# Image stores of the weight stage: twelve pieces, one in each of steps 6 to 17, in place of six in a row

## The chip, the core and the metric

The kernel runs on one core of one Trainium2 chip. The metric is the device time of one execution in microseconds (us), from the first to the last instruction of the program. Three timed executions of the kernel before gave 1593.47, 1605.23 and 1599.48 us, a median of 1599.48 us.

## What is computed

A tower of three layers on 16 images of 3 x 112 x 112. Only the first layer, the patch tokenizer, touches the change. Cut to what matters here:

```python
# x: 16 x 3 x 112 x 112 -> 784 patches of 3 x 16 x 16
x = (x - mean) / (1e-06 + std)           # per patch and colour, ddof=1
x = x / sqrt(16)
x = conv2d(x, conv1_w, conv1_b)          # 3 -> 64 channels, 3x3
residual = x
x = gelu(group_norm(x, gn1_g, gn1_b))
x = conv2d(x, rconv1_w, rconv1_b)        # 64 -> 64
x = gelu(group_norm(x, gn2_g, gn2_b))
x = conv2d(x, rconv2_w, rconv2_b)        # 64 -> 64
x = residual + x
x = conv2d(x, proj_w, proj_b, stride=16) # 64 x 16 x 16 -> 192: one token per patch
tokens = x + row_emb[...] + col_emb[...]
# then an attention layer and a two-branch transformer layer on the tokens
```

The last 3x3 convolution is linear and is followed by a linear projection, so the kernel folds rconv2_w into proj_w once, before it touches a patch. It also folds the projection with conv1_w, for the residual path.

## The kernel before

The program has three stages: the **weight stage** (the first 246 us), the **patch stage** (conv1, norm, gelu, conv, norm, gelu and projection over 784 patches, two in flight, in seven groups), and the tail with the attention and transformer layers. Each engine runs its own stream of instructions, and the streams meet at semaphores.

**The weight stage** folds 192 output channels in 24 steps (FU = 24) of 8 channels (U = 8). Step n works in one of two halves of everything, p = n % 2. In the order in which the data go through it:

- SyncE (SP), `fold_io` (L227): waits until VectorE has split step n's weights (`s_psp`, L230), loads the projection weights of step n + 2 into the stage that this frees (`load_proj`, L215 and L216: `sb_f32q` for even steps, a part of `sb_arena` for odd ones), waits until ScalarE has evacuated step n's second product (`s_tev`, L232), and stores it to DRAM (`scratch_fold`) with two DMAs (L234).
- VectorE (DVE), `proj_split` (L675): waits for the load, and for TensorE to be through with step n - 2 (`s_tps`, L679); writes the weights as an fp16 high part (L682) and an fp16 rest (L684) into `sb_acts`.
- TensorE (PE), `fold_step` (L504): waits for the split of step n (L506), does 36 matmuls of 512 columns (L476) and 18 of 192 columns (L517).
- ScalarE (ACT), `fold_step` (L389): moves the results out of PSUM (L393, L400).
- VectorE, `w_lo` (L686, L691): the low part of the folded weights. On VectorE the order is w_lo of step n - 2, split of step n, w_lo of step n - 1, split of step n + 1 (`fold_pair`, L709). Its first splits and its work on the image (L700 to L735) stand among them.

Two buffers hold the weights on their way in, two the split weights, two each result.

**The image** is loaded once as `xt` (112 partitions, 3 colours, 7 patches of 256 numbers, fp32), normalised by VectorE in place (`s_xch` counts to 42), and split into 12 padded fp16 planes `xhl`, 6 of high parts and 6 of rests (`s_xhl` counts to 13). SyncE writes both back to DRAM. `xt` goes to `scratch_x` with three DMAs (L244), one for each colour. `xhl` goes to `x_planes` with three DMAs (L247) of six planes each: high parts, rests, high parts again. Eight small DMAs (L252) then store zeros from `sb_arena` behind the last patch of the 18 planes. All fourteen count up `s_scr`. When it has its full 14 x 16 (L263), SyncE reads the first patches back with `load_im` (L254, L256), for units 0 and 1, two DMAs each, into `sb_im`. VectorE waits for the same count at L757 before it lets the patch stage reuse the image's buffers.

**Order on SyncE before.** The queue is one stream, written out by hand: `fold_io` of steps 0 to 5 as a hardware loop (`Fori(0, 3)`), then the six image stores and the eight zero stores in a row, then `fold_io` of steps 6 to 21 as a second hardware loop, then the wait on `s_scr` and the four loads of `sb_im`, then `fold_io` of steps 22 and 23 without a load, then the store of the low weights (L269), and then the patch stage.

TensorE starts the patch stage with `conv1` (L535, L536) after waits on `s_im`, on VectorE's memsets of first rows (`s_rowz`, L763), and on the last evacuations of the weight stage (L629 to L634). It needs unit 1 in `sb_im` at the third conv1 (L638).

Of the kernel before, what the change touches and what calls it, by code (L numbers as in the profile page):

```python
# [22 lines left out]
B, C, P, CH, E = 16, 3, 16, 64, 192  # L23
HP = 7
ROWS = B * HP
NPAT = ROWS * HP
SL, WD = 9, 18
PAD = SL * WD
# [7 lines left out]
FU = E // U  # L36
RUN = (U - 1) * PAD + 8 * WD + P
PLANE = (NPAT + 3 * U + 1) * PAD
# [11 lines left out]
W_READY = 10  # L50
HB = U * PAD + WD
MID = 48
MEANS_AT, CONV1_AT = 10, 13


# [14 lines left out]
def build_front(nc, a, emb, xs, ts, wrd):  # L70
# [7 lines left out]
    scr = nc.dram_tensor("x_planes", (18, PLANE), F16)  # L78
    wlod = nc.dram_tensor("w_lo", (128, HALF * E), F16)
    with ExitStack() as ctx:  # L80
# [3 lines left out]
        def sem(name):  # L84
            return ctx.enter_context(nc.semaphore(name))
# [46 lines left out]
        n = 2 * C * 7 * 256  # L132
        xt = b0[0:ROWS, 0:n].bitcast(F32).rearrange("p (c w n) -> p c w n", c=C, w=7)
        xhl = b0[0:ROWS, n:n + 12 * 7 * PAD].rearrange("p (q n) -> p q n", q=12)
# [26 lines left out]
        s_cst, s_xvar, s_xstd, s_xz, s_xhl, s_xch = (sem("constants"), sem("x_var"), sem("x_std"), sem("x_zeroed"),  # L161
                                               sem("x_split"), sem("x_chain"))
        s_scr, s_zero, s_padz = sem("x_stored"), sem("zero_tile"), sem("pads_zeroed")
# [42 lines left out]
        def _(sp):  # L206
# [8 lines left out]
            def load_proj(n, p):  # L215
                sp.dma_start(stage[p], a["proj"][:, bass.ds(n * (U * DENSE), U * DENSE)]).then_inc(s_pld[p], 16)  # L216
# [10 lines left out]
            def fold_io(i, p, last):  # L227
                n = 2 * i + p
                if not last:
                    sp.wait_ge(s_psp, 2 * n + 2)  # L230
                    load_proj(n + 2, p)
                sp.wait_ge(s_tev, 3 * n + 3)  # L232
                for h in range(2):
                    sp.dma_start(bass.AP(tensor=ts.tensor, offset=n * (U * TR * DENSE) + h * (Q * TR * DENSE),  # L234
                                         ap=[[DENSE, TR], [TR * DENSE, Q], [1, DENSE]]),
                                 tev[p][TP * h:TP * h + TR, :, :]).then_inc(s_ts[p], 16)

            with sp.Fori(0, 3) as i:
                for p in range(2):
                    fold_io(i, p, False)  # L240

            sp.wait_ge(s_xch, 42)
            for c in range(C):
                sp.dma_start(xs.rearrange("(r w) (c n) -> r c w n", w=7, c=C)[:, c], xt[:, c]).then_inc(s_scr, 16)  # L244
            sp.wait_ge(s_xhl, 13)
            for k, h in enumerate((0, 1, 0)):
                sp.dma_start(bass.AP(tensor=scr, offset=k * 6 * PLANE, ap=[[7 * PAD, ROWS], [PLANE, 6], [1, 7 * PAD]]),  # L247
                             xhl[:, 6 * h:6 * h + 6, :]).then_inc(s_scr, 16)
            sp.wait_ge(s_zero, 1)
            for n, k in ((NPAT, U), (NPAT + U, U), (NPAT + 2 * U, U), (NPAT + 3 * U, 1)):  # L250
                for at, planes in ((0, 12), (12, 6)):
# [2 lines left out]
            def load_im(u, p):  # L254
                for up in range(2):
                    sp.dma_start(im[p][54 * up:54 * up + 54, 0:RUN],  # L256
                                 bass.AP(tensor=scr, offset=u * (U * PAD) + up * WD,
                                         ap=[[1, 3], [PLANE, 18], [1, RUN]])).then_inc(s_im[p], 16)

            with sp.Fori(3, FU // 2 - 1) as i:  # L260
                for p in range(2):
                    fold_io(i, p, False)
            sp.wait_ge(s_scr, 16 * 14)  # L263
            load_im(0, 0)
            load_im(1, 1)
            for p in range(2):
# [201 lines left out]
        def _(pe):  # L468
# [79 lines left out]
            def project(b, n0, n1):  # L548

                for n in range(n0, n1):  # L550
                    c = max(k for k in range(NCH) if CHS[k] <= n)
                    to_low = (HALF + (c % 2) * WCH + n - CHS[c] - n) * E
                    both = bass.AP(tensor=wall, offset=n * E, ap=[[WALL, 128], [to_low, 2], [1, E]])
                    tiles = ((0, 0), (64, MID))
                    for at, k in tiles:
# [96 lines left out]
        def _(dve):  # L652
# [13 lines left out]
            n = 4  # L666
# [61 lines left out]
            for q in range(6):  # L728
                c, pr = q // 2, q % 2
# [24 lines left out]
            ins.then_inc(s_padz, 1)  # L754
            dve.wait_ge(s_tps, FU)
            dve.wait_ge(s_padz, 3)
            dve.wait_ge(s_scr, 16 * 14)  # L757
            v.sem_inc(s_rd, 1)
            v.sem_inc(s_pjr, 1)
            v.sem_inc(s_sp2, 2)  # L760
# [125 lines left out]
            n = 2  # L886
# [714 lines left out]
```

## Time and profile before

| | us |
|---|---|
| three timed executions | 1593.47, 1605.23, 1599.48 |
| their median | 1599.48 |
| the profiled execution's own time | 1601.61 |
| its span, first to last instruction | 1599.8 |
| TensorE busy in the span | 1455.8 (91%) |
| VectorE, ScalarE, GpSimd busy | 1136.8, 841.1, 582.9 |

The profile is one execution. In it each engine has a busy time, and for idle time the trace names what the engine waited for. "SPq" is SyncE's queue: the time that SyncE spends on issuing a DMA, not the transfer. "DMA share" is the mean busy share of the core's 16 DMA engines. "PEclk" is the TensorE clock that was granted, as a share of full speed. "[14.34 <-DVE sb_acts L684]" at the end of a row says that the engine sat idle for 14.34 us and that an instruction of VectorE released it.

### The profile page before, as it was taken

The numbers are of one execution on the slowest core, as the hardware profiler recorded it, in microseconds if no ns is written. First come the engines' busy times: TensorE is split into PE (matmuls) and PEld (weight loads), VectorE is DVE, ScalarE is ACT, GpSimd is POOL, SyncE is SP. The second block draws the span as 40 slices with busy tenths as digits, with TensorE's granted clock in tenths as the row PEclk, the third lists the DMA queues.
The fourth block names the chain that finished last, engine by engine and source line by source line (L and its number), as shares of the span: only waits on it lengthen the run. The fifth ranks groups of instructions, "written<-read, shape, count | busy, mean of one in ns | idle before, by whom it ended". The sixth has DMA issues, their size and how long they took to land. (4 is left out here: it accounts for less than half of the span.)

```text
span 1599.8 us, 42535 instructions
## 1 busy us (share of the span) xinstructions
PE 1455.8 (91%) x13394; PEld 1029.1 (64%) x13394; DVE 1136.8 (71%) x4230; ACT 841.1 (53%) x2118; POOL 582.9 (36%) x1111
## 2 busy tenths in 40 slices
PE   6969996888999999999999998999999487899999
PEld 2424442333688588768867885886788486565747
DVE  7724335999888988888888888888888622383710
ACT  1212223777767776666776776677776302323442
POOL 2000003555544544545555554545444201242500
PEclk9989997999999999999999999999999797967999
DMA  6463325433555455445545554554555758000000
GB/s 179 130 196 89 101 88 214 105 99 97 148 147 144 123 147 136 132 125 146 143 124 146 143 134 119 147 145 119 149 147 142 208 152 183 1 1 1 1 2 14
DMA packets 117216, 190.62 MB, mean 119 GB/s; under 512 B 18251, under 2 KB 86282, under 8 KB 116940
## 3 DMA queue, kind: packets, MB, share of 16 engines
q1 hardware_dynamic: 117068, 188.60, 43.1%
q8 instruction: 98, 1.61, 0.4%
q14 instruction: 50, 0.41, 0.1%
HBM read 103.34 MB, written 21.30 MB: 78 GB/s over the span
## 5 line engine op out<-in xcount | busy, mean ns | idle before, releaser
L363 POOL TENSOR_TENSOR sb_tmp<-sb_mst,sb_half_neg 128x8 f32<-128x8 f32 x200 | 354.6, 1773 | 681.1 <-DVE sb_mst L789 681.1
L501 PE MATMUL rc<-sb_acts,sb_rwd 128*64 128x512 f16 x1764 | 562.8, 392 | 16.3 <-DMA sb_acts<-sb_hst 15.8
L502 PE MATMUL rc<-sb_acts,sb_rwd 128*64 128x512 f16 x1764 | 563.7, 392 | 0.0
L417 ACT ACTIVATE sb_f32q<-c,sb_gsh,sb_gsc 128x128 f32<-128x128 f32 x792 | 298.8, 459 | 282.6 <-POOL sb_gsh L373 282.6
L501 PE MATMUL rc<-sb_acts,sb_rwl 128*64 128x512 f16 x1176 | 364.2, 392 | 5.5 <-issue 5.5
L502 PE MATMUL rc<-sb_acts,sb_rwl 128*64 128x512 f16 x1176 | 363.7, 391 | 0.0
L556 PE MATMUL pj<-sb_wall,sb_arena 128*64 128x384 f16 x1792 | 310.0, 336 | 21.9 <-DMA sb_wall<-w_lo 15.3
L425 ACT ACTIVATE sb_g2f<-rc,sb_gsh,sb_gsc 128x128 f32<-128x128 f32 x784 | 298.2, 483 | 4.5 <-POOL sb_gsh L373 4.5
L560 PEld LDWEIGHTS pj<-sb_wall,sb_arena 128*64 128x64 f16 x1792 | 219.2, 222 | 63.4
L560 PE MATMUL pj<-sb_wall,sb_arena 128*64 128x192 f16 x1792 | 240.6, 246 | 0.0
L556 PEld LDWEIGHTS pj<-sb_wall,sb_arena 128*64 128x64 f16 x1792 | 215.4, 218 | 39.0 <-DMA sb_wall<-w_lo 16.8
L501 PEld LDWEIGHTS rc<-sb_acts,sb_rwd 128*64 128x64 f16 x1764 | 179.8, 110 | 75.2 <-DMA sb_acts<-sb_hst 24.7
L476 PE MATMUL rc<-sb_acts,sb_arena 128*128 128x512 f16 x864 | 196.4, 385 | 29.6 <-DVE sb_acts L684 29.6
L502 PEld LDWEIGHTS rc<-sb_acts,sb_rwd 128*64 128x64 f16 x1764 | 179.7, 110 | 6.0
L768 DVE BATCH_NORM_STATS2 sb_bn<-rc 128x6 f32<-128x128 f32 x784 | 173.6, 284 | 11.9 <-issue 5.4
L768 DVE BATCH_NORM_STATS2 sb_bn<-c 128x6 f32<-128x128 f32 x800 | 174.3, 278 | 0.5 <-PE c L536 0.5
L476 PEld LDWEIGHTS rc<-sb_acts,sb_arena 128*128 128x128 f16 x864 | 81.9, 97 | 135.7 <-issue 34.8
L501 PEld LDWEIGHTS rc<-sb_acts,sb_rwl 128*64 128x64 f16 x1176 | 126.7, 109 | 47.4 <-issue 10.5
L808 DVE TENSOR_TENSOR sb_arena<-sb_g2f,sb_arena 128x512 f32 (+1 forms) x196 | 135.7, 693 | 28.7 <-issue 18.2
L801 DVE TENSOR_TENSOR sb_acts<-sb_f32q,sb_hst 128x512 f16<-128x512 f32 x198 | 137.9, 696 | 6.8
L433 ACT ACTIVATE sb_arena<-sb_g2f 128x512 f32 (+1 forms) x196 | 125.0, 638 | 26.0 <-ACT sb_g2f L425 8.6
L502 PEld LDWEIGHTS rc<-sb_acts,sb_rwl 128*64 128x64 f16 x1176 | 126.8, 109 | 0.5
(162 smaller groups left out, 1786.0 us busy)
## 6 DMA issues: line engine op xcount, KB each, us to landing
sb_acts<-sb_hst SPq DMA_DIRECT2D x792, 78.8 KB, 2.6
sb_wall<-w_lo SPq DMA_DIRECT2D x56, 528.0 KB, 3.8
sb_im<-x_planes SPq DMA_DIRECT2D x202, 136.5 KB
sb_wall<-w_lo SPq DMA_DIRECT2D x28, 480.0 KB, 3.7
sb_f32q<-in_proj SPq DMA_DIRECT2D x12, 576.0 KB, 4.0
sb_arena<-in_proj SPq DMA_DIRECT2D x12, 576.0 KB, 4.5
w_lo<-sb_arena SPq DMA_DIRECT2D x1, 6144.0 KB, 17.3
scratch_fold<-sb_wall SPq DMA_DIRECT2D x48, 123.8 KB
```

Of the source, the lines that this page charges most:

```text
L363: ch.did(gp.tensor_tensor(t1, var, half_neg[:, :], ALU.pow))
L417: ins = nc.scalar.activation(g1f[:, q * Q + m, :], c1[q][:, m * HALF:(m + 1) * HALF], ACT.Gelu, bias=gsh[q][:, m:m + 1], scale=gsc[q][:, m ...
L425: ins = nc.scalar.activation(g2f[:, q * Q + m, :], rc[p][q][:, m * HALF:(m + 1) * HALF], ACT.Gelu, bias=gsh[q][:, Q + m:Q + m + 1], scale= ...
L433: nc.scalar.activation(g2[:, buf, 0, bass.ds(slot, Q), :], g2f[:, q * Q:q * Q + Q, :], ACT.Copy).then_inc(s_sp2h, 1)
L476: last = nc.tensor.matmul(out, w[:, wp, 3 * t + m, :], v[:, xp, t:t + 8, m * Q:(m + P) * Q], start=(n == 0), stop=(n == 17))
L501: nc.tensor.matmul(out[0:CH, :], w_odd, x_odd, start=(n == 0), stop=(n == 14))
L502: yield nc.tensor.matmul(out[CH:128, :], w_even, x_even, start=(n == 0), stop=(n == 14))
L556: last = nc.tensor.matmul(pj[at:at + 64, 0:2 * E], g2[:, b, 0, k:k + 64, n], both, start=(n == 0), stop=False)
L560: last = nc.tensor.matmul(pj[at:at + 64, 0:E], g2[:, b, 1, k:k + 64, n], whi[:, n, :], start=False, stop=(n == HALF - 1))
L768: v.bn_stats(bn6[s][:, at + m, :], src[:, m * HALF:(m + 1) * HALF]).then_inc(s_dch, 1)
L801: v.tensor_tensor(lo, src, hi, ALU.subtract).then_inc(s_sp1, 1)
L808: v.tensor_tensor(lo, src, hi, ALU.subtract).then_inc(s_sp2, 1)
```

## The change

SyncE's second and third parts are merged into one list. `fold_io` of steps 0 to 21 is written out as straight code with constants, where two hardware loops stood. After `fold_io` of each step from 6 to 17 one piece of the image is stored, twelve in all:

- pieces 0 to 2 (steps 6 to 8): the three colours of `xt`, the same three DMAs as before, with the wait on `s_xch` ahead of the first;
- pieces 3 to 11 (steps 9 to 17): `xhl`, two planes at a time, nine DMAs in place of three, with the wait on `s_xhl` ahead of the first of them.

The eight zero stores, unchanged, now stand behind `fold_io` of step 21, directly ahead of the wait on `s_scr` and of the four loads of `sb_im`. The count that `s_scr` must reach, on SyncE and at L757 on VectorE, grows from 14 to 20 times 16. Nothing is changed on the other engines.

```diff
-            with sp.Fori(0, 3) as i:
-                for p in range(2):
-                    fold_io(i, p, False)
-
-            sp.wait_ge(s_xch, 42)
-            for c in range(C):
-                sp.dma_start(xs.rearrange("(r w) (c n) -> r c w n", w=7, c=C)[:, c], xt[:, c]).then_inc(s_scr, 16)
-            sp.wait_ge(s_xhl, 13)
-            for k, h in enumerate((0, 1, 0)):
-                sp.dma_start(bass.AP(tensor=scr, offset=k * 6 * PLANE, ap=[[7 * PAD, ROWS], [PLANE, 6], [1, 7 * PAD]]),
-                             xhl[:, 6 * h:6 * h + 6, :]).then_inc(s_scr, 16)
+            def store_piece(m):
+                if m < C:
+                    if m == 0:
+                        sp.wait_ge(s_xch, 42)
+                    sp.dma_start(xs.rearrange("(r w) (c n) -> r c w n", w=7, c=C)[:, m], xt[:, m]).then_inc(s_scr, 16)
+                else:
+                    if m == C:
+                        sp.wait_ge(s_xhl, 13)
+                    k, q = (m - C) // 3, 2 * ((m - C) % 3)
+                    sp.dma_start(bass.AP(tensor=scr, offset=(6 * k + q) * PLANE, ap=[[7 * PAD, ROWS], [PLANE, 2], [1, 7 * PAD]]),
+                                 xhl[:, 6 * (k % 2) + q:6 * (k % 2) + q + 2, :]).then_inc(s_scr, 16)
+
+            for n in range(FU - 2):
+                fold_io(n // 2, n % 2, False)
+                if 6 <= n < 6 + PIECES:
+                    store_piece(n - 6)
             sp.wait_ge(s_zero, 1)
             for n, k in ((NPAT, U), (NPAT + U, U), (NPAT + 2 * U, U), (NPAT + 3 * U, 1)):
...
-            with sp.Fori(3, FU // 2 - 1) as i:
-                for p in range(2):
-                    fold_io(i, p, False)
-            sp.wait_ge(s_scr, 16 * 14)
+            sp.wait_ge(s_scr, 16 * (PIECES + 8))
             load_im(0, 0)
             load_im(1, 1)
             for p in range(2):
...
             dve.wait_ge(s_padz, 3)
-            dve.wait_ge(s_scr, 16 * 14)
+            dve.wait_ge(s_scr, 16 * (PIECES + 8))
```

## Rows read from the trace of the kernel before

**Rows 1.** Windows of the weight stage: stretch, length, busy time of each engine, clock, DMA
```profile
80.50:94.60 14.10, 7.18 (x47) 3.31 (x45) 0.00 (x0) 1.97 (x5) 0.00 (x0) 0.93 0.95 315
94.60:99.70 5.10, 0.00 (x0) 0.00 (x0) 0.00 (x0) 0.00 (x0) 0.00 (x0) 0.50 0.68 180
...
112.86:245.90 133.04, 132.72 (x812) 61.49 (x810) 49.53 (x59) 29.83 (x77) 0.00 (x0) 1.00 0.31 90
```

**Rows 2.** Timeline of SyncE's queue, steps 5 to 7: start, time to issue, line
```profile
69.81 0.78 SPq L234 DMA_DIRECT2D scratch_fold<-sb_wall  x2
70.80 3.24 SPq L244 DMA_DIRECT2D scratch_x<-sb_arena  x3
74.08 6.38 SPq L247 DMA_DIRECT2D x_planes<-sb_arena  x3
80.51 13.81 SPq L252 DMA_DIRECT2D x_planes<-sb_arena  x8
94.69 1.04 SPq L216 DMA_DIRECT2D sb_f32q<-in_proj  x1
```

**Rows 3.** Timeline of TensorE and VectorE, start of steps 7, 8 and 9
```profile
78.77 8.04 PE L476 MATMUL rc<-sb_acts,sb_arena 128*128 128x512 f16 x36
99.72 0.76 DVE L682 TENSOR_SCALAR sb_acts<-sb_f32q 128x1152 f16<-128x1152 f32 x1 [20.17 <-DMA sb_f32q<-in_proj]
102.01 10.04 PE L476 MATMUL rc<-sb_acts,sb_arena 128*128 128x512 f16 x36 [14.34 <-DVE sb_acts L684]
...
112.86 5.42 PE L476 MATMUL rc<-sb_acts,sb_arena 128*128 128x512 f16 x24
```

**Rows 4.** Timeline of an undisturbed step, SyncE and VectorE
```profile
140.45 0.77 SPq L234 DMA_DIRECT2D scratch_fold<-sb_wall  x2
141.85 0.38 SPq L216 DMA_DIRECT2D sb_f32q<-in_proj  x1
148.93 0.75 DVE L682 TENSOR_SCALAR sb_acts<-sb_f32q 128x1152 f16<-128x1152 f32 x1
```

**Rows 5.** Lines L216, L244, L247, L252, L224: issue in ns, min/median/max; L216's landing
```profile
DMA to landing us min/median/max: 3.7/4.3/6.6
...
L244 SPq DMA_DIRECT2D scratch_x<-sb_arena x3: 641/676/1829, 70.8 to 72.2; - x3
L247 SPq DMA_DIRECT2D x_planes<-sb_arena x3: 1787/1804/2703, 74.1 to 77.8; - x3
L252 SPq DMA_DIRECT2D x_planes<-sb_arena x8: 343/1374/4992, 80.5 to 94.0; - x8
L224 SPq DMA_DIRECT2D sb_w1s<-sb_arena x6: 737/738/907, 11.9 to 19.7; - x6
```

**Rows 6.** DMA issues by line: KB each (the page's last part, and the same for 0 to 260)
```profile
sb_acts<-sb_hst SPq DMA_DIRECT2D x792, 78.8 KB, 2.6
...
x_planes<-sb_arena SPq DMA_DIRECT2D x3, 1488.4 KB
scratch_x<-sb_arena SPq DMA_DIRECT2D x3, 784.0 KB
```

**Rows 7.** Timeline of the end of the weight stage, step 21's store to the first conv1
```profile
228.88 0.77 SPq L234 DMA_DIRECT2D scratch_fold<-sb_wall  x2
229.86 3.09 SPq L256 DMA_DIRECT2D sb_im<-x_planes  x4
236.67 8.04 PE L476 MATMUL rc<-sb_acts,sb_arena 128*128 128x512 f16 x36
248.35 0.38 PE L535 MATMUL c<-sb_im,sb_w1s 108*64 108x512 f16 x1 [2.78 <-DVE sb_acts L763]
256.62 0.60 PE L535 MATMUL c<-sb_im,sb_w1s 108*64 108x512 f16 x1 [3.80 <-ACT sb_f32q L417]
```

**Rows 8.** Windows of one us: sb_im's drain, of which two of ten
```profile
235.00:236.00 1.00, 1.00 (x10) 0.41 (x10) 0.00 (x0) 0.02 (x1) 0.00 (x0) 1.00 0.20 78
...
240.00:241.00 1.00, 1.00 (x6) 0.44 (x5) 0.00 (x0) 0.10 (x1) 0.00 (x0) 1.00 0.20 62
```

More of the change, by code:

```diff
@@ L52 @@
 MID = 48
+PIECES = 12
 MEANS_AT, CONV1_AT = 10, 13
```

## The prediction, made before the run

> **What bounds the kernel now.** I read the page first, for where TensorE, which is busy for 91% of the span, is not. Of the stretches with a low digit, one lies inside the weight stage, around 100 us. The windows of that stage say how large it is: between 94.6 and 99.7 us no engine does anything while the DMA engines still move 180 GB/s, and in the 14.1 us before it TensorE is busy for 7.18 only; later, from 112.86 to 245.9, it is busy for 132.72 of 133.04 us [rows 1]. So the stage is bound by TensorE wherever it runs freely, and once it was not.
>
> The timeline of TensorE and VectorE shows the hole. Step 7 begins at 78.77, step 8 only at 102.01, after 14.34 us of idling that a split of VectorE ended; VectorE itself had waited 20.17 us for the load of step 8 [rows 3]. The timeline of SyncE's queue says why this load was late: behind the fold stores of step 5 stand three stores of 784 KB, three of 1488 KB and eight small ones, and the load comes at 94.69 [rows 2, 6]. The small ones took 13.81 us to issue, one of them 4.99 and the quickest 0.34 [rows 2, 5]: such a spread for nearly equal work says that SyncE was held by a full queue. The bytes agree: 3 x 784 + 3 x 1488.4 KB are 6.98 MB, at the 315 GB/s of the window [rows 1] 22.2 us, from 70.8 to 93.0. The load is issued just after.
>
> **The length of a free step.** Step 9 begins at 112.86 and step 23 at 236.67 [rows 3, 7]: 123.81 us for 14 steps, 8.84 each.
>
> **What the change removes.** The load of step 8 no longer stands behind the stores; it is issued at about 70.7, behind step 5's fold stores [rows 2], and with the 4.3 us that a load takes to land [rows 5] it is there at 75. Step 8 can then begin 8.84 after step 7, at 87.61, and step 9 at 96.45 where it began at 112.86. That is 16.4 us. It has two parts: the idle 14.34, and 2.0 us by which the 36 matmuls of step 8 were slower after the hole, 10.04 for 8.04 [rows 3]. The granted clock in the hole was 0.50, the lower level of 1.2 GHz, and 1.00 in the long free stretch [rows 1]; without the idling nothing lowers it here. What bounds next is TensorE itself.
>
> **What it adds in each of steps 6 to 17.** Steady order, from an undisturbed step: fold store at 140.45, load at 141.85, the split that uses this load at 148.93, which is 7.08 us after its issue [rows 4]. TensorE wants that split one step later still. Its steps begin at 112.86 + k x 8.84, so at 148.23 and 157.07; from the start of a split to the matmuls takes 2.29 us (99.72 to 102.01) [rows 3]. The load must therefore have landed by 157.07 - 2.29 = 154.78, 12.9 us after its issue. A piece is put between fold store and load:
>
> - A piece of `xt` (three of them): issue 0.68 us [rows 5], 0.803 MB at 315 GB/s 2.5 us ahead of the load, which lands 4.3 after its issue: 7.5 us. That is 0.4 us late for VectorE, 5.4 early for TensorE. Cost nothing.
> - A piece of two planes (nine): a third of 1.80, 0.6 us [rows 5], 0.508 MB or 1.6 us, with the load 6.5. Cost nothing.
> - Bounds. From below: nothing, as a store that nobody waits for can't give time. From above, the dearest row for each term: issue 1.83, 0.803 MB at the 180 GB/s of the last window 4.5 us, landing 6.6 [rows 1, 5], in all 12.9 us, just what there is. So it is hidden there too.
> - Behind the waiting split in VectorE's queue stands w_lo of the step before, which frees a bank that TensorE takes two steps later; 0.4 us matter no more there. If the cover were gone, each microsecond beyond the 12.9 would be a microsecond of TensorE once, and again in each step only if a whole step's transfers took over 8.84 us. A free step moves 90 GB/s x 8.84 = 0.80 MB [rows 1]; with a piece of `xt` 1.60 MB, 5.1 us at 315 GB/s.
> - The wait on `s_xch` and `s_xhl` ahead of pieces 0 and 3: VectorE had done both when SyncE came there at 70.8 and 74.08 [rows 2]. No wait.
> - SyncE's own time: 0.77 + 0.38 + 0.68 of 8.84 us. The straight code drops some register work; nothing on the path.
>
> The Trainium skill, DMA: Bandwidth & Descriptors, section Bandwidth (Measured), speaks against cutting: it wants DMAs of 1 MiB or more, and gives each a fixed part of about 2.0 us beside bytes at 436 GB/s. By that rule, an estimate, six stores would take 12 + 16 = 28 us and twelve 24 + 16 = 40. The trace has the six in about 22 us, so it did not add a fixed part for stores that stand in a row. What the cutting would cost if it did is the second rival below.
>
> **What it moves: the eight zero stores, to the end.** This is the part with a price. Before, SyncE went from the fold store of step 21 (228.88 + 0.77) straight to the four loads of `sb_im` at 229.86, and TensorE's first conv1 came at 248.35, released by VectorE [rows 7]. Afterwards all of this is 16.4 earlier: fold store done at 213.2, conv1 due at 231.9, the third conv1, which needs unit 1, at 256.62 - 16.4 = 240.2. In between now stand the zero stores, their landing (the wait on `s_scr`) and the loads:
>
> - Eight zero stores. Bounds: 8 x 0.34 = 2.7 us and the 13.81 of before [rows 2, 5]. The nearest row without a full queue is a DMA of 12 short rows, 0.74 [rows 5]; I take 8 x 0.74 = 5.9.
> - Landing of the last: nearest row 2.6 us, from issue to landing of a small DMA [rows 6]; bounds 0 and the 6.6 of the slowest projection load [rows 5].
> - The loads drain at 78 GB/s and the last row that shows them is 240 to 241 [rows 8], so unit 1 is there 11 us after 229.86. Half of their 546 KB, 0.28 MB, takes 3.6 us at this rate, so unit 0 is there after 7.4.
>
> Sum: 213.2 + 0.2 + 5.9 + 2.6 + 7.4 = 229.3 for unit 0, due at 231.9: 2.6 us early. Unit 1: 232.9, due at 240.2. Cost nothing. With the zero stores at 13.81: 237.2, 5.3 late; with the landing at 6.6 as well 241.2, 9.3 late. The fold stores of steps 22 and 23 and the store of the low weights stand behind; step 22's is due at 237.6 - 16.4 = 221.2 and SyncE is free at about 225, but no engine waits for its buffer any more, and step 23's is due at 230. VectorE comes to L757 at about 231, when `s_scr` is full.
>
> The patch stage and the tail start earlier and are otherwise untouched.
>
> **The sum.** 1599.8 - 16.4 = 1583.4 by the span of the profiled execution; its own time, 1601.61, is 1.8 longer, and the median of the runs shown, 1599.48, is 0.3 under its span. From the median: 1599.48 - 16.4 = **1583.1 us**.
>
> **The rivals.**
>
> 1. *The end of the stage gives some back.* If a zero store costs by its shape what it cost in the row (1.73 each), and not by the full queue, conv1 waits for `sb_im`: 1583.1 + 5.3 = 1588.4, with the slow landing 1592.4. It decides from 5.9 + 2.6 = 8.5 us for all eight. For it: the zero stores are few rows with few engines, and the order is now a chain. Against it: the quickest took 0.34.
> 2. *The cutting costs a fixed part for each piece.* Six more DMAs at the 2.6 us of a small one [rows 6] are 15.6 us; if they came onto the path, 1583.1 + 15.6 = 1598.7. This is the rule of the skill's page at work. Against it: 5.4 us of slack in each step, used afresh each time.
> 3. *The DMA engines become the bound (slower).* Steps 6 to 17 then last as long as their transfers. It costs more than the 16.4 gained once the excess over 8.84 us is (16.4 + 5.4) / 12 = 1.8 us a step, so 10.6 us for 1.60 or 1.30 MB, under 151 and 122 GB/s. At 100 GB/s: 3 x 7.2 + 9 x 4.2 - 5.4 = 54 us, 1583.1 + 54 = 1637. Against it: the engines moved 315 GB/s of the same stores.
> 4. *The change doesn't do what it says:* the load of step 8 is late for another reason too and the hole stays, 1599.5. Against it: the row that released the split is that load, issued last of a full queue.
>
> **Chances.** The forecast 0.81; rival 1 0.11; rival 2 0.03; rival 3 0.02; rival 4 0.03. Three runs of before lie within 12 us, so a median may be off by some 4 either way. The forecast's own range is 1577 to 1589. To 1591 it takes in most of rival 1, and 1575 gives the scatter room below: 1575 to 1591. About 1% is what a measurement of this kernel can tell from no change; that line is at 1583.5 and the forecast lies 0.4 us beyond it. So the forecast's chance is split nearly in half, and all of rivals 1, 2 and 4 falls within 1%: faster 0.46, same 0.52, slower 0.02.
>
> **What would show it.** Right: TensorE without a gap from step 6 to step 23; step 8's matmuls at 8.04 us and a clock of 1.00 around 100 us; no wait of VectorE for a projection load over a microsecond; the weight stage ends 16.4 us earlier, at 229.5; eight zero stores issued in under 8 us around 213 to 220, first conv1 released by VectorE, not by a DMA. Wrong: TensorE waiting for `sb_im` at 232 (rival 1); VectorE waiting for loads in each of steps 9 to 20 (rivals 2, 3); the hole at 100 us still there (rival 4); or the patch stage longer than before by several us, which nothing here foresees.

## The result, and the profile after

| | before | changed |
|---|---|---|
| timed executions, median of 20 | 1603.47 us | 1586.68 us |
| their lowest and highest | 1590.8 to 1609.34 | 1574.34 to 1593.95 |
| profiled execution, span | 1599.8 | 1577.5 |
| first conv1 of the patch stage | 248.35 | 232.55 |
| last conv1 of the patch stage | 1248.9 | 1233.7 |

The changed kernel takes 0.990 of the time of before, 95% interval 0.9877 to 0.9923. In the medians that is 16.8 us; the sum said 16.4. Where it lies can be read off three views.

The timeline of TensorE and VectorE, changed kernel (start, duration, line; a wait and its releaser in brackets):

```profile
79.38 8.04 PE L479 MATMUL rc<-sb_acts,sb_arena 128*128 128x512 f16 x36
88.22 8.03 PE L479 MATMUL rc<-sb_acts,sb_arena 128*128 128x512 f16 x36
88.93 0.75 DVE L685 TENSOR_SCALAR sb_acts<-sb_arena 128x1152 f16<-128x1152 f32 x1
...
232.55 0.38 PE L538 MATMUL c<-sb_im,sb_w1s 108*64 108x512 f16 x1 [2.77 <-DVE sb_acts L766]
```

Step 8 now begins 8.84 us after step 7, without a wait, and its matmuls take 8.03 us. Before it began 23.24 later and took 10.04 [rows 3]. The first conv1 is still released by VectorE, 15.8 us earlier. This execution had been 0.61 us late before the change comes in (step 7 at 79.38, before at 78.77), so the stage itself is 16.41 us shorter.

SyncE's queue, changed kernel: a step with a colour, a step with two planes, and the end of the stage.

```profile
80.28 0.72 SPq L235 DMA_DIRECT2D scratch_fold<-sb_wall  x2
81.05 0.69 SPq L243 DMA_DIRECT2D scratch_x<-sb_arena  x1
81.78 0.64 SPq L217 DMA_DIRECT2D sb_arena<-in_proj  x1
...
106.82 0.72 SPq L235 DMA_DIRECT2D scratch_fold<-sb_wall  x2
107.58 0.40 SPq L248 DMA_DIRECT2D x_planes<-sb_arena  x1
108.02 0.46 SPq L217 DMA_DIRECT2D sb_f32q<-in_proj  x1
...
212.94 0.72 SPq L235 DMA_DIRECT2D scratch_fold<-sb_wall  x2
213.70 2.82 SPq L258 DMA_DIRECT2D x_planes<-sb_arena  x8
217.80 3.07 SPq L262 DMA_DIRECT2D sb_im<-x_planes  x4
```

A piece takes 0.4 to 0.7 us to issue, and the next load follows at once. The eight zero stores, which took 13.81 us in the row [rows 2], take 2.82.

The waits in the stretch from 60 to 232 us, changed kernel (engine, line, who is waited for: us in total, times, longest), and the landing of the 24 projection loads:

```profile
PEld c L520 <- issue: 8.1, 19, 0.4
ACT sb_wall L403 <- PE pj L520: 3.8, 20, 0.2
PEld rc L479 <- issue: 1.3, 1, 1.3
PE rc L479 <- DVE sb_acts L687: 1.1, 1, 1.1
```

```profile
DMA to landing us min/median/max: 3.7/5.6/7.0
```

VectorE doesn't wait for any load. The one wait of TensorE is the 1.1 us of step 6 (the row that begins with PE and not PEld), where VectorE is late with the image; it was there before. The pieces do slow the loads, from a median of 4.3 us [rows 5] to 5.6, and that is hidden.

The span of the profiled execution fell by 22.3 us, 6.5 more than the first conv1. The patch stage ends 15.2 us earlier, and the other 7.1 lie in the tail, where the granted clock was 0.89 in this execution and 0.86 in that of before. A second profile of the changed kernel has its last conv1 at 1234.6 and a span of 1587.1: the same stages, and a tail 8.7 us longer than in its first profile, with a clock of 0.85. So two executions of one kernel differ there by as much, and the 7.1 us can't be put down to the change.

### The profile page after: what moved, and what is told of

The parts are those of the page before. It is cut to its first block and busy times, and to the rows that moved or that the text cites. A ratio compares the mean times of both kernels' runs of the same rounds, so it can differ in the third digit from the quotient of the medians.

```text
span 1577.5 us, 42341 instructions
## 1 busy us (share of the span) xinstructions
PE 1441.6 (91%) x13394; PEld 1018.7 (65%) x13394; DVE 1137.4 (72%) x4230; ACT 838.7 (53%) x2118; POOL 581.8 (37%) x1111
## 5 line engine op out<-in xcount | busy, mean ns | idle before, releaser
L559 PE MATMUL pj<-sb_wall,sb_arena 128*64 128x384 f16 x1792 | 310.2, 337 | 22.4 <-DMA sb_wall<-w_lo 15.8
```

Of the source, the lines that this page charges most:

```text
L559: last = nc.tensor.matmul(pj[at:at + 64, 0:2 * E], g2[:, b, 0, k:k + 64, n], both, start=(n == 0), stop=False)
```

## The experiments

The theory to be tested: a load lands only when what was queued ahead of it has been moved; TensorE notices if that is later than 12.9 us after its due issue; spreading the stores keeps it below, and neither the cutting nor the place of the zero stores matters. The rivals: the cutting does it; the zero stores were the stall; DMAs have a fixed price. All stretches of TensorE named "hole" are idle time ahead of step 8, if no other step is named. Where no ratio is given, a kernel was executed once, and only its timeline is read. Where stores stay whole, the code's `PIECES` is 6, and `store_large(m)` in the code shown below stands for its `store_piece(m)`: m from 0 to 2 is a colour, m from 3 to 5 six planes.

### Cutting without spreading

```diff
             for n in range(FU - 2):
                 fold_io(n // 2, n % 2, False)
-                if 6 <= n < 6 + PIECES:
-                    store_piece(n - 6)
+                if n == 5:
+                    for m in range(PIECES):
+                        store_piece(m)
```

> The twelve pieces in a row after step 5, the zero stores at the end of the stage: the cutting without the spreading. Theory of the bytes: the load of step 8 still stands behind 6.98 MB, 22.2 us at 315 GB/s, so it lands at 95 to 97 and the hole in TensorE stays at 9 to 12 us; it shrinks by 2 to 5 us, since the zero stores no longer stand in between. Kernel 0.3% faster than before. Rival, short pieces free the queue: hole under 3 us, kernel 1% faster. Rival, a fixed part of 2 us for each DMA: twelve pieces take 12 us longer than six, hole 20 us or more, slower than before.

Timed against before: 0.9999 (0.996 to 1.0038). Its timeline, of SyncE's queue and then of TensorE:

```profile
73.28 15.76 SPq L248 DMA_DIRECT2D x_planes<-sb_arena  x9
89.08 1.73 SPq L217 DMA_DIRECT2D sb_f32q<-in_proj  x1
...
100.12 10.74 PE L480 MATMUL rc<-sb_acts,sb_arena 128*128 128x512 f16 x36 [12.76 <-DVE sb_acts L688]
```

The hole is 12.76 us, a little over the 9 to 12 expected, and the load lands at 97.7, later than the 95 to 97; the matmuls behind the hole are 2.7 slow. In the time, cutting alone brings nothing that can be told from no change. The nine plane pieces take 15.76 us to issue where the same nine, spread, take 0.38 to 0.40 each: SyncE was held by the queue. A fixed 2 us for each DMA isn't there either, since the load lands 1.9 us earlier in the timeline than before, not 12 later.

### Spreading without cutting

```diff
-                    k, q = (m - C) // 3, 2 * ((m - C) % 3)
-                    sp.dma_start(... offset=(6 * k + q) * PLANE, ap=[..., [PLANE, 2], ...]), xhl[:, 6 * (k % 2) + q:6 * (k % 2) + q + 2, :])
+                    k = m - C
+                    sp.dma_start(... offset=k * 6 * PLANE, ap=[..., [PLANE, 6], ...]), xhl[:, 6 * (k % 2):6 * (k % 2) + 6, :])
```

> The six large stores uncut, one in each of steps 6 to 11, the zero stores at the end: the spreading without the cutting. Theory: a store of six planes is 1.52 MB, 4.8 us at 315 GB/s ahead of the load, which lands about 11 us after its issue was due, against 12.9 us of room. No hole, the same gain as the twelve pieces, 1% faster than before, first conv1 at 232 to 233 us. Rival, the cutting is needed: TensorE waits 1 to 3 us in each of steps 11 to 14, half the gain or less.

Timed: 0.9898 (0.9862 to 0.9935), the changed kernel's gain. First conv1 at 232.89. The slowest load landed 9.5 us after its issue, 9.3 after the issue was due, where about 11 was expected:

```profile
DMA to landing us min/median/max: 3.8/4.8/9.5
```

VectorE waited for loads three times, 5.8 us in all, TensorE never. So the spreading is what gains, and the cutting is not needed.

### The zero stores: last behind a row, or early ahead of spread pieces

Row of six large stores after step 5, zero stores at the end:

```diff
             for n in range(FU - 2):
                 fold_io(n // 2, n % 2, False)
+                if n == 5:
+                    for m in range(6):
+                        store_large(m)
             sp.wait_ge(s_zero, 1)
```

> Six large stores in a row after step 5 as before, only the eight zero stores moved to the end, the queue written out straight. Theory: the 13.81 us of the zero stores were the full queue and not their own price; taking them away leaves the bytes, hole 9 to 12 us where 14.3 stood, 0.3% faster than before, like the twelve pieces in a row. Rival, the zero stores were the stall: the hole shrinks by 13.8 us to nothing and all of the gain is there.

```profile
80.68 4.96 SPq L217 DMA_DIRECT2D sb_f32q<-in_proj  x1
85.68 4.08 SPq L235 DMA_DIRECT2D scratch_fold<-sb_wall  x2
89.80 2.35 SPq L217 DMA_DIRECT2D sb_arena<-in_proj  x1
92.19 5.75 SPq L235 DMA_DIRECT2D scratch_fold<-sb_wall  x2
...
104.48 10.73 PE L480 MATMUL rc<-sb_acts,sb_arena 128*128 128x512 f16 x36 [16.49 <-DVE sb_acts L688]
```

Both theories missed. The load of step 8 is issued 14 us earlier than before, at 80.68 for 94.69 [rows 2], and yet the hole is larger, 16.49 for 14.34 [rows 3]; the load takes 21.4 us to land. The time is 1.0024 (0.9984 to 1.0064), which is not told apart from before. That the zero stores were not the stall stands; that fewer things in the row would shorten it does not. The next two runs and a table go into why.

Pieces spread as in the change, zero stores ahead of them, after step 5:

```diff
                 fold_io(n // 2, n % 2, False)
+                if n == 5:
+                    <the eight zero stores>
                 if 6 <= n < 6 + PIECES:
```

> The twelve pieces spread over steps 6 to 17, but the zero stores back behind step 5, ahead of them. Theory: with no full queue they issue in 2.8 us, hidden in the step; the time is that of the changed kernel within 0.3%, and the loads of sb_im are issued about 4 us earlier, at 213.8 and not 217.8, which changes nothing. Rival, their place matters: a wait of VectorE for the load of step 8 of over 2 us appears.

```profile
70.92 2.79 SPq L257 DMA_DIRECT2D x_planes<-sb_arena  x8
73.76 0.36 SPq L217 DMA_DIRECT2D sb_f32q<-in_proj  x1
```

The eight issue in 2.79 us in the very place where they took 13.81 [rows 2]; the price was the queue's. First conv1 at 232.44, no wait of VectorE for a load. From step 7 to the first conv1 it takes 153.19 us, the change 153.17. The ratio, 0.9939 (0.9907 to 0.9971), is 0.4% above the change's where 0.3% was expected at most, but the intervals overlap, and the weight stage shows no difference that would explain it.

### Why the row costs more without the zero stores

Before, with SyncE's loops written out and nothing moved, in short:

```diff
-            with sp.Fori(0, 3) as i:
-                for p in range(2):
-                    fold_io(i, p, False)
+            for n in range(6):
+                fold_io(n // 2, n % 2, False)
```

(and the second loop likewise, for steps 6 to 21)

> The kernel before with SyncE's two hardware loops written out as straight code and nothing moved. It tells two readings of the larger hole (16.5 us) of the row with the zero stores last apart. If the zero stores, by holding SyncE, kept fold stores and the next load out of the queue while the slow DMA engines finished, the hole is back at 14.3 us here. If the straight code is the cause, it is 16 us or more here too.

```profile
81.06 14.45 SPq L259 DMA_DIRECT2D x_planes<-sb_arena  x8
95.56 0.48 SPq L217 DMA_DIRECT2D sb_f32q<-in_proj  x1
...
102.41 10.65 PE L480 MATMUL rc<-sb_acts,sb_arena 128*128 128x512 f16 x36 [14.01 <-DVE sb_acts L688]
```

The hole is back at 14.01 us, so the straight code does not make it larger. With the zero stores in the row, it is 2.5 us shorter than without.

The load of step 8 ahead of the row:

```diff
                 if n == 5:
+                    sp.wait_ge(s_psp, 14)
+                    load_proj(8, 0)
                     for m in range(6):
                         store_large(m)
```

> Six large stores in a row after step 5, zero stores at the end, but the load of step 8 is issued ahead of the row instead of behind it. Theory (a load lands only when the slowest DMA engine has worked off all that was queued ahead): step 8 begins without a wait; now the load of step 9 stands behind the row and lands at 98 to 102 as the load of step 8 did, where TensorE wants it by 94; a hole of 6 to 10 us ahead of step 9, first conv1 at 240 to 243 us. Rival, it was the one load that was lost: no hole, first conv1 at 232 to 233.

```profile
81.58 8.03 SPq L255 DMA_DIRECT2D scratch_fold<-sb_wall  x2
89.65 1.54 SPq L217 DMA_DIRECT2D sb_arena<-in_proj  x1
91.24 5.61 SPq L235 DMA_DIRECT2D scratch_fold<-sb_wall  x2
...
107.73 10.81 PE L489 MATMUL rc<-sb_acts,sb_arena 128*128 128x512 f16 x36 [11.08 <-DVE sb_acts L697]
```

Step 8 begins in time, at 87.74, and the hole moves to step 9, 11.08 us; expected were 6 to 10. The load of step 9 landed at 105.4, later than the 98 to 102 expected, and the first conv1 came at 246.0, where 240 to 243 was expected.

The trace also holds every DMA packet with its start, duration and size, and the sizes tell the transfers apart: 2268 bytes for the planes, 4608 for a projection load. All times are us from the span's start; "landed" is issue plus landing time of the load that TensorE waited for:

```
                               load     first load    last plane   load
                               issued   packet        packet done  landed
before                         94.7     96.4          97.0         99.6
loops written out              95.6     96.6          97.3         100.0
cut, in a row                  89.1     91.9          95.5         97.7
row, zero stores last          80.7     91.0          100.3        102.1
row, load of step 8 ahead      89.7     92.2          102.5        105.4
```

In all five the load lands 1.8 to 2.9 us after the last packet of the planes, whenever it was issued. In the fourth, some DMA engines had begun on the load 9.4 us before others were through with the planes. So the row isn't one queue that is worked off at 315 GB/s; the load is complete when the slowest DMA engine has got through its share. The Trainium skill, DMA: Bandwidth & Descriptors, says in the section on why a DMA increments its semaphore by 16 that the engines of a DMA finish independently and that only the full count means landed; the trace agrees: the sixteen increments for this load come between 92.7 and 102.1 us in the fourth, and between 98.7 and 99.6 before.

The table also shows what I had missed. With the uncut row and no zero stores behind it, SyncE gets fold stores and a load into the queue earlier, and then the last plane packet itself is later, 100.3 and 102.5 for 97.0 and 97.3, although the planes were issued in the same three DMAs within a microsecond of the same time. The cut row is an exception: it too has a load and fold stores behind it, from 89.1 on, and its last plane packet is at 95.5. The windows show the extra traffic, first before, then the row with the zero stores last:

```profile
91.00:95.00 4.00, 0.00 (x0) 0.00 (x0) 0.00 (x0) 0.00 (x0) 0.00 (x0) 0.69 0.71 205
95.00:99.00 4.00, 0.00 (x0) 0.00 (x0) 0.00 (x0) 0.00 (x0) 0.00 (x0) 0.50 0.68 173
```

```profile
91.00:95.00 4.00, 0.00 (x0) 0.00 (x0) 0.00 (x0) 0.00 (x0) 0.00 (x0) 0.74 0.98 238
95.00:99.00 4.00, 0.00 (x0) 0.00 (x0) 0.00 (x0) 0.00 (x0) 0.00 (x0) 0.50 0.83 282
```

My reading is that the engines that are through with the planes take bandwidth from those that aren't. The durations of the packets bear this out: between 83 and 91 us a plane packet takes 106 to 110 ns on average in all five; of those that start between 93 and 95 us it takes 110 and 112 in the first two kernels, 143 in the cut row, and 290 and 242 in the last two. So the late plane packets are slow where other transfers run beside them. What they share, which engines are late and why is not shown, since no record names the engine of a packet.

### How much one step can hold

One colour and six planes in each of steps 6, 7 and 8:

```diff
-                if 6 <= n < 6 + PIECES:
-                    store_piece(n - 6)
+                if 6 <= n < 9:
+                    store_large(n - 6)
+                    store_large(n - 3)
```

> One colour and six planes (0.80 + 1.52 MB) in each of steps 6, 7 and 8: where the room of 12.9 us runs out. Theory of the room: issue 0.8, 2.33 MB at 315 GB/s 7.4, landing 4.3, in all 12.5 us for the first load, and 1.1 us more for each next since 3.13 MB take 9.9 us in a step of 8.84; TensorE waits 0 to 4 us in all, the rest of the gain stays, 0.8 to 1% faster than before. Rival, any queue with over 2 MB in a step stops the stage: a hole of 8 us or more.

```profile
107.29 8.03 PE L480 MATMUL rc<-sb_acts,sb_arena 128*128 128x512 f16 x36 [0.94 <-DVE sb_acts L688]
118.17 9.70 PE L480 MATMUL rc<-sb_acts,sb_arena 128*128 128x512 f16 x36 [1.98 <-DVE sb_acts L688]
```

TensorE waits 0.94 and 1.98 us, and the matmuls behind the second are 1.7 slow, at a granted clock of 0.82: 4.6 us in all, the first conv1 at 237.65. Timed 0.9944 (0.9912 to 0.9975). Counted from its due issue (1.4 us after the start of the fold store, [rows 4]), the load of step 9 lands after 11.9 us (issued at 82.85, 11.1 to land, due at 82.06), and TensorE doesn't notice. That of step 10 lands after 13.9 (92.32 + 12.5, due at 90.91): 1.0 over the room of 12.9, and TensorE waits 0.94. So the room was right to a tenth. The growth from step to step was worked out worse: 1.1 us by the bytes, and 2.0 and 2.2 in fact (the load of step 11 lands 16.1 us after its due issue).

Two more stores to DRAM of their own in each of steps 9 to 17, beside the piece:

```diff
+                if 9 <= n < 6 + PIECES:
+                    sp.dma_start(<six planes of xhl -> extra>).then_inc(s_scr, 16)
+                    sp.dma_start(<one colour of xt -> extra>).then_inc(s_scr, 16)
```

> The changed kernel with two more stores, to DRAM of their own, in each of steps 9 to 17: six planes and a colour, 2.33 MB a step beside the piece. Theory: 3.63 MB a step at 315 GB/s take 11.5 us and a step only 8.84, so nine steps lose 2.7 us each, 24 us in all less up to 4 us of room, TensorE waits 18 to 24 us and the kernel gives back all of its gain: the DMA engines bind from 2.8 MB a step. Rival, fixed parts and full queues cost more than bytes: 40 us or more.

```profile
152.03 9.55 PE L486 MATMUL rc<-sb_acts,sb_arena 128*128 128x512 f16 x36 [3.17 <-DVE sb_acts L694]
165.73 9.52 PE L486 MATMUL rc<-sb_acts,sb_arena 128*128 128x512 f16 x36 [3.28 <-DVE sb_acts L694]
180.57 10.61 PE L486 MATMUL rc<-sb_acts,sb_arena 128*128 128x512 f16 x36 [4.45 <-DVE sb_acts L694]
```

In its one execution, 1630.71 us, the first conv1 is at 276.11, 43.6 later than in the change, where TensorE was expected to wait 18 to 24. TensorE waits 31.4 - 1.1 = 30.3 us, and the matmuls of seven of the nine late steps take 9.5 to 10.6 us, together about 12.8 too many. The eight steps from 125.38 to 235.44 take 13.76 us each. With 3.63 MB a step that is 264 GB/s (the window has 262, at a DMA share of 0.89), not 315, and the lower clock, 0.84 and 0.75 in the matmuls at 138.5 and 180.57, costs what the sum had left out. That is the 40 us or more of the rival, but a fixed part for each DMA is not shown by it, and why the rate is 264 stays open. So the mechanism of the prediction's rival 3 exists, and it sets in between 2.3 MB a step, where the uncut spread showed nothing on TensorE, and 3.1 MB, where the three full steps cost 4.6 us.

### The end of the stage

Zero stores, their wait and the loads of `sb_im` behind the fold store of step 23:

```diff
+            for p in range(2):
+                fold_io(FU // 2 - 1, p, True)
             <the eight zero stores>
             sp.wait_ge(s_scr, 16 * (PIECES + 8))
             load_im(0, 0)
             load_im(1, 1)
-            for p in range(2):
-                fold_io(FU // 2 - 1, p, True)
```

> Zero stores, the wait for them and the loads of sb_im all behind the last fold store (step 23, at 231.4 us). Theory: 231.4 + 2.8 + 1.3 + 7.4 = 243 us for unit 0, first conv1 about 10 us later than in the changed kernel (232.55), released by a DMA. Rival, sb_im is there much sooner than the 7.4 us that were worked out from its drain: 3 to 6 us later only.

```profile
235.25 3.07 SPq L257 DMA_DIRECT2D sb_im<-x_planes  x4
...
242.09 0.61 PE L538 MATMUL c<-sb_im,sb_w1s 108*64 108x512 f16 x1 [12.60 <-DMA sb_im<-x_planes]
```

The first conv1 is 9.5 us later than in the change, and a DMA releases it, as expected. Unit 0 is there 6.8 us after its loads are issued. In the change they are issued at 217.80, so, if they take as long there, it is there by 224.6, 7.9 us early.

### The store of the low weights in eight parts

In the patch stage SyncE copies each unit's activations from `sb_hst` into `sb_acts` with four DMAs, the doublings. In the change the first of them stand behind one store of 6.3 MB.

```diff
-            sp.dma_start(wlod.ap(), b1[:, 0:HALF * E]).then_inc(s_wst, 16)
...
                         double(2 * u + 3, 1 - p, 1)
+                        if first and 2 * j + p < 8:
+                            lo = (2 * j + p) * (HALF // 8) * E
+                            sp.dma_start(wlod.ap()[:, lo:lo + HALF // 8 * E], b1[:, lo:lo + HALF // 8 * E]).then_inc(s_wst, 16)
```

(the waits on `s_wst` grow to 128)

> The changed kernel, with the 6.3 MB store of the low weights in eight parts, one behind each of the first eight units of the patch stage, where one large store stood ahead of the first. Theory: the first doublings of sb_acts (issue 4.85 us, TensorE waiting 3.3 us for their data) no longer stand behind 6.3 MB, and the patch stage gains 3 to 6 us, 0.2 to 0.4%. Rival: each part of 0.79 MB now delays one unit's doublings by 2.5 us, eight times, and the time is the same or up to 10 us longer.

For comparison, the changed kernel once more:

> The changed kernel itself, timed beside the one with the low weights' store in eight parts. All theories: 0.990 of the kernel before. The profile shows how far two executions of one kernel differ in the tail (its clock was 0.89 there, 0.86 in the profile of before): 2 to 7 us.

And the eight parts once more:

> The low weights' store in eight parts again, with more rounds and on the same chip as the changed kernel. Theory: the third conv of the patch stage stays 3 to 4 us earlier, and the time is 0.2% under the changed kernel's. Rival, from its first profile: sb_acts is now waited for more often (8.7 us in 9 times, where it was 4.7 in 3), the lead is gone by the end of the patch stage and the two take the same time.

Against before, the eight parts took 0.9895 (0.9838 to 0.9952) the first time. The second time, on the same chip as the changed kernel, they took 0.9883 (0.9836 to 0.9931), and the changed kernel 0.9885 (0.985 to 0.992). The waits of TensorE from 232 to 420 us, first the changed kernel (second profile), then the eight parts (second profile):

```profile
PE rc L504 <- DMA sb_acts<-sb_hst: 6.1, 5, 3.7
```

```profile
PE rc L506 <- DMA sb_acts<-sb_hst: 8.9, 10, 1.6
```

The long first wait is gone, and ten short ones stand in place of five. A conv1 that comes at 253.69 in the changed kernel comes at 250.36, 3.3 us earlier, as expected; but the last conv1 is at 1236.5, in the changed kernel at 1234.6, so the lead is gone by then, as the rival had it. No gain can be told from the times. That each part delays other doublings fits the waits, and no run isolates it.

## Why the prediction was right

**The hole.** It was to close whole, idle time and slow matmuls, 14.34 + 2.0 us. It did: 16.41 us in the profile, 16.8 in the medians. 1583.1 us was worked out from a median of 1599.48; from that of the 20 runs, 1603.47, the same sum gives 1587.1 for a measured 1586.68. The interval of the ratio leaves both sides of the 1% line open, as the near even split of the chances had it.

**The pieces in the steps.** Hidden, as forecast. Each term was somewhat dear: issue 0.40 for the 0.6 of a plane piece, and the load landed at most 7.0 us after its due issue for 7.5. VectorE wasn't late at all, where 0.4 us were worked out. The 12.9 us of room are borne out from both sides by the first two landings of the three-step run.

**The zero stores at the end.** Cost nothing, as forecast, with more to spare than worked out: issue 2.82 us for 5.9, the wait for their landing 1.3 for 2.6, unit 0 after 6.8 for 7.4; 7.9 us early in place of 2.6. The price of 0.74 each was taken from a row that is nearest in shape; the lower bound, 0.34, was the true one (2.82 / 8 = 0.35), and the quickest of the eight rows had shown it.

**The rivals.** 1 (the end gives some back) was ruled out by the change's own trace, and moving the chain 17.4 us later showed that such a wait would have been real. 2 (a fixed part for each piece) is ruled out by the cut row and by the uncut spread; the prediction's own argument against it was a misreading, as told below. 3 (the DMA engines bind) has its place, above 2.3 MB a step, where the change has at most 1.6. 4 fell with the hole.

**The step that held only by luck.** The prediction said that the load was late because 6.98 MB at 315 GB/s stood ahead of it, and that "the load is issued just after". The fit is luck: the last plane packet of before is done not at 93.0 but at 97.0, 26.2 us after the row began. The windows have 345 to 349 GB/s from 83 to 91 us and 205 from 91 to 95; the engines did not finish together. As a mechanism the sum is too simple. It gave 9 to 12 us for the row without the zero stores and 6 to 10 for the row behind one load, and 16.49 and 11.08 were measured; for nine steps of 3.63 MB it gave 24 us, and the first conv1 came 43.6 later. What holds in its place: the end of the slowest DMA engine decides, and what is queued behind an uncut row is not free. For the change itself this made no difference, since no step's queue is deep.

The same 22 us stand in the prediction's argument against a fixed part for each DMA. "The trace has the six in about 22 us" is the sum and not the trace. The trace has 26.2, close to the 28 that the prediction works out with a fixed part, so the six alone don't tell against it. What tells against a fixed part is the cut row: twelve stores in 25.3 us (70.1 to 95.5), where the prediction's estimate with a fixed part is 40. The Trainium skill, DMA: Bandwidth & Descriptors, has the fixed part of about 2.0 us in its section on the anatomy of one DMA on the SWDGE path, as a fit to that path, and not under Bandwidth, as the prediction says; here SyncE issues the stores.

## What to carry to other kernels

Large stores that nobody waits for belong one to a step between the loads of a running pipeline; work out how long after its due issue a load may land (here 12.9 us, counted through all the buffers and not only to the first engine that waits), and keep the bytes put ahead of it below that. Cutting stores of up to 1.5 MB smaller added nothing here once they were spread. A DMA that seems dear to issue should be compared with the same DMA where the queue is empty before its price is moved elsewhere in a sum.

## What was not expected of the hardware

- Tiny DMAs behind the row of large stores held the issuing engine for long: 13.81 us for eight [rows 2], against 2.79 and 2.82 us where no such row was ahead.
- With the zero stores taken out of the row, the load behind it was issued 14 us earlier and landed 2.5 us later (99.6 and 102.1).
- DMA engines that share one row of stores drift apart: some began on the load at 91.0 us while others were at the planes until 100.3, with the row issued from 70.8 on. Plane packets then took 290 ns where 110 was usual.
- The clock after short waits of TensorE. Behind waits of 0.51, 0.94 and 1.83 us the 36 matmuls took 8.03 us, at a granted clock of 1.00. Behind one of 1.98 us they took 9.70, at 0.82, so in part at the lower level of 1.2 GHz. Behind 3.1 to 5.6 us they took 9.5 to 10.6, and behind 11 to 16 us 10.6 to 10.8, at 0.74 or 0.75; before, behind 14.34 us, 10.04 [rows 3] at 0.79. That the length of the wait alone decides is not shown.
